# An attention layer with a hand-written step table: pv after the job in seven steps, a new job order, a max pass one step shorter ahead, and a prologue that fills rows from two DMA queues

## The chip, the cores and the metric

The kernel runs on one core of a Trainium2 chip. The metric is the time of one execution on the device in microseconds (us). Three runs of the kernel before gave 575.6 (median), 574.88 and 576.89.

## The reference

Eight batches of 512 tokens with 256 features, 16 heads of 16. Cut to what matters:

```python
xn = layer_norm(x, norm_w, norm_b)
q = (xn @ q_w + q_b).reshape(8, 512, 16, 16)
k = (xn @ k_w + k_b).reshape(8, 512, 16, 16)
att = einsum('bnhl,bmhl->bnmh', q, k)
att = att + (1.0 - mask.reshape(8, 1, 512, 1)) * -1000000.0
att = softmax(att, axis=2)
v = ((xn @ v_w + v_b) * mask[:, :, None]).reshape(8, 512, 16, 16)
y = einsum('bnmh,bmhl->bnhl', att, v).reshape(8, 512, 256)
e = silu(cond) @ emb_w + emb_b
scale, shift = split(e[:, None, :], 2, axis=2)
h = layer_norm(y, sb_norm_w, sb_norm_b) * (1.0 + scale) + shift
return x + silu(h) @ out_w + out_b
```

## The kernel before

A batch is 16 steps (`STEPS`): four groups of four heads, and for each group four chunks of 128 keys. The program runs ten bodies: body -1 is the prologue, body b computes the attention of batch b, body 8 is the tail. Each engine has its own instruction list, and semaphores tie them.

In a step TensorE does, in this order (`body`, L550): two score matmuls (`st_unit` 0 and 1, L442: the first pair), where it is due the turn of the maxima (`max_turn`, L434), the product of the exponentials of the step before with the values (`pv_step`, L459: "pv"; four heads side by side in four column strips of the array), four matmuls of the max pass (`max_quad`, L408: "maxima"; two at a time in two row strips), two further scores (the second pair), and one job (`job`, L499). The scores have two PSUM banks in turn, so a score waits until the exponential of the score two before it has been read (`exp_done`).

The softmax takes its row maxima from the max pass. It runs `MAX_LEAD` = 7 steps ahead of the scores with a cheaper product of split bf16 parts. VectorE reduces each pair of max banks (`max_pair`, L724). After four steps the sixteen columns of maxima of a group are turned by TensorE (`TURNS`: steps 1, 5, 9, 13), split into two bf16 parts (`split_max`, L759) and put by DMA into two rows of `q_rows` (`place_max`, L1140), so that the score matmul itself subtracts them.

`JOBS` names the sixteen jobs of a body as (kind, index, batch offset). Long jobs are the four projections of Q and K (`proj`), two value projections (`vproj`) and two output products (`outp`). Short ones are transposes: of the normed x (`xturn`), of y (`yturn`) and of the normed y (`hturn`). All use one bank, `job_ps`; a job waits until the last one has been read (`bank_freed`, L339).

ScalarE (L577) takes the four exponentials of a step and reads jobs: a projection twice, in full precision after the step's last exponential (`qk_full`) and rounded, as part 0, after the second exponential of the next step (`qk_parts`). It also copies `pv_ps` into `y_t` once in four steps. GpSimd subtracts part 0 (`take_rest`), VectorE rounds part 1 (`late_job`, whose places are in `LATE`), GpSimd makes part 2. SyncE issues all the DMAs (`spread`, L1101): it saves four copies of the parts to DRAM, fills three mask rows of each half, waits until the copies have landed and issues eight DMAs that fill the rows of K and Q for the group.

```python
JOBS = [
    ("yturn", 3, -1), ("xturn", 0, 1), ("xturn", 1, 1), ("proj", 0, 1),
    ("hturn", 0, -1), ("vproj", 0, 1), ("yturn", 0, 0), ("proj", 1, 1),
    ("hturn", 1, -1), ("vproj", 1, 1), ("yturn", 1, 0), ("proj", 2, 1),
    ("yturn", 2, 0), ("outp", 0, -1), ("outp", 1, -1), ("proj", 3, 1),
]
```

The prologue loads x and the weights, norms x, splits the mask into three bf16 parts on VectorE (`mask_rows`, L681), projects groups 0 to 3 of batch 0 and runs the max pass of its first seven steps. `keep_warm` issues matmuls on zeros in between.

Of the kernel before, what the change touches and what calls it, by code (L numbers as in the profile page):

```python
# [47 lines left out]
MAX_LEAD = 7  # L48
# [23 lines left out]
    ("yturn", 3, -1), ("xturn", 0, 1), ("xturn", 1, 1), ("proj", 0, 1),  # L72
    ("hturn", 0, -1), ("vproj", 0, 1), ("yturn", 0, 0), ("proj", 1, 1),
    ("hturn", 1, -1), ("vproj", 1, 1), ("yturn", 1, 0), ("proj", 2, 1),
    ("yturn", 2, 0), ("outp", 0, -1), ("outp", 1, -1), ("proj", 3, 1),
]

FIRST_JOBS = {1: 1, 2: 2, 3: 3, 5: 5, 6: 7, 7: 9, 8: 11, 15: 15}

TURNS = {1: 1, 5: 2, 9: 3, 13: 4}  # L80

LATE = {(2, 0): (15, -1), (5, 0): (3, 0), (7, 2): (4, 0), (9, 0): (7, 0), (10, 2): (8, 0), (13, 0): (11, 0)}
LATE_FIRST = {(5, 0): (3, 0), (8, 0): (7, 0), (12, 0): (11, 0)}
X_STAT = {(11, 0): (0,), (11, 2): (1,), (12, 2): (2,), (14, 2): (3,), (15, 2): (4,)}
Y_STAT = {(2, 1): (0,), (2, 2): (1,), (3, 0): (2, 3, 4)}
X_STAT_FIRST = 8


TURN_OF = {3: 1, 0: 5, 1: 9, 2: 13}
# [3 lines left out]
WARM_FIRST = {3: 4, 7: 6, 8: 2}  # L93
# [63 lines left out]
def attention_layer(nc, x, cond, mask, norm_w, norm_b, q_w, q_b, k_w, k_b, v_w, v_b,  # L157
                    emb_w, emb_b, sb_w, sb_b, out_w, out_b, out):
    with ExitStack() as ctx:
# [163 lines left out]
        def emptied(kind, i, batch):  # L323
            if kind == "proj":
                return part0_ready, NG * batch + i + 1
            if kind == "yturn":
# [6 lines left out]
                    ("proj", 2): st_ps[0][:, :], ("proj", 3): pv_ps[:, :]}  # L333
# [33 lines left out]

        block = ctx.enter_context(nc.Block())
# [3 lines left out]
        def _(pe):  # L372
# [14 lines left out]
            keep_warm(pv_ps, 7)  # L387
# [71 lines left out]
            def pv_step(b, t):  # L459
# [5 lines left out]
                if c == 0:  # L465

                    pe.wait_ge(v_ready, NG * b + g + 1)
                    wait(pe, yt_ready, NG * b + g)
                    if isinstance(b, int) and b == 0 and g == 0:

                        pe.wait_ge(part0_ready, NG)
# [27 lines left out]
            def job(t, b):  # L499
# [4 lines left out]
                if isinstance(b, int) and b == 0 and t == 1:  # L504

                    pe.wait_ge(setup_done, 1)
# [70 lines left out]
        def _(act):  # L577
# [15 lines left out]
            def read_job(b, t, half):  # L593
# [5 lines left out]
                if kind == "proj" and half == 1:  # L599
                    wait(act, copies_saved, 16 * COPIES * (NG * d + i))  # L600
# [31 lines left out]

            def yt_copy(b, t):
# [10 lines left out]
            def body(b):  # L644
                for t in range(STEPS):
# [7 lines left out]
                    read_job(b, t, 0)  # L653

# [21 lines left out]
        def _(dve):  # L676
            dve.memset(warm_in[:, :].bitcast(F32), 0.0).then_inc(warm_ready, 1)  # L677

            dve.memset(k_rows[0:HALF + P // 4, 0:NG // 2, :, :].bitcast(F32), TWO_ONES)

            def mask_rows():  # L681

                dve.wait_ge(mask_loaded, 16)
                dve.tensor_scalar(mask_bias[:, :], mask_in[:, :], -1.0, MASKED, ALU.add, ALU.mult).then_inc(setup_chain, 1)
                dve.wait_ge(setup_chain, 2)
                dve.tensor_copy(mask_parts[:, 0, :], mask_bias[:, :]).then_inc(setup_chain, 1)
                dve.wait_ge(setup_chain, 3)
                dve.tensor_tensor(mask_rest[:, 0, :], mask_bias[:, :], mask_parts[:, 0, :], ALU.subtract).then_inc(setup_chain, 1)
                dve.wait_ge(setup_chain, 4)
                dve.tensor_copy(mask_parts[:, 1, :], mask_rest[:, 0, :]).then_inc(setup_chain, 1)  # L690
                dve.wait_ge(setup_chain, 5)
                dve.tensor_tensor(mask_rest[:, 1, :], mask_rest[:, 0, :], mask_parts[:, 1, :], ALU.subtract).then_inc(setup_chain, 1)
                dve.wait_ge(setup_chain, 6)
                dve.tensor_copy(mask_parts[:, 2, :], mask_rest[:, 1, :]).then_inc(maskp_ready, 1)

                dve.memset(k_rows[0:HALF + P // 4, NG // 2:NG, :, :].bitcast(F32), TWO_ONES).then_inc(k_preset, 1)

            def silu_of_cond():
# [4 lines left out]
                dve.wait_ge(setup_chain, 1)  # L703
# [3 lines left out]
                                ).then_inc(mask_col_ready, 1)  # L707

# [189 lines left out]
            def body(b):  # L898
# [6 lines left out]
                for t in range(STEPS):  # L905
# [12 lines left out]
                    if t == 0 and isinstance(b, int) and b == 0:  # L918
                        embedding()
# [275 lines left out]
```

## Time and profile before

| | |
|---|---|
| median of three runs | 575.6 us |
| the profiled execution | 575.16 us |
| its span in the profile | 573.4 us |
| TensorE busy (PE) | 527.0 us, 92% |
| VectorE (DVE) | 414.9 us, 72% |
| ScalarE (ACT) | 366.3 us, 64% |
| GpSimd (POOL) | 197.2 us, 34% |
| granted TensorE clock, mean | 0.99 |

Busy times are sums over the span, and matmul ends are modelled, so a busy TensorE is not one at its peak. In the rows further down a line of a timeline gives start, length, engine, source line, operation, what is written and read, how many instructions were merged, and in brackets the idle time before them with what ended it.

### The profile page before, as it was taken

What the parts mean: (1) busy time and instruction counts of PE and PEld (TensorE: products, weight loads), DVE (VectorE), ACT (ScalarE), POOL (GpSimd) and SP (SyncE); (2) the same over time, 40 slices, a digit from 0 to 9 for tenths busy, and PEclk for the clock granted to TensorE, in tenths of its full rate; (3) what the DMA queues carried; (4) which work ended last, traced back from release to release, by engine and by line L of the source; (5) the groups of instructions that cost most, each with busy time, mean ns of one, the idle gap of its engine ahead of it and who ended that gap; (6) DMA issues with size and microseconds to landing.
All of it is one profiled execution on the core that took longest, in us unless ns stands there. A gap on an engine that the chain in (4) does not pass through costs nothing.

```text
span 573.4 us, 9986 instructions
## 1 busy us (share of the span) xinstructions
PE 527.0 (92%) x2841; PEld 194.4 (34%) x2845; DVE 414.9 (72%) x658; ACT 366.3 (64%) x674; POOL 197.2 (34%) x240
## 2 busy tenths in 40 slices
PE   7878999899999999999999999999999999988886
PEld 2433233223333233433333333433333333412243
DVE  7467767787687877887787877887777877787325
ACT  2302766677766877577766877577856877576851
POOL 9333203245322623255322623154322622132003
PEclk9979999999999999999999999999999999999999
DMA  5443243224424342424324342424424322421021
GB/s 144 164 131 92 82 134 95 86 83 123 120 75 149 90 123 86 127 78 128 111 76 148 93 124 80 130 76 128 120 65 147 95 91 76 152 59 49 1 74 37
DMA packets 55050, 57.95 MB, mean 101 GB/s; under 512 B 12376, under 2 KB 42200, under 8 KB 55024
## 3 DMA queue, kind: packets, MB, share of 16 engines
q1 hardware_dynamic: 55024, 57.64, 33.5%
q8 instruction: 12, 0.20, 0.1%
q14 instruction: 14, 0.11, 0.1%
HBM read 36.35 MB, written 21.00 MB: 100 GB/s over the span
## 4 chain that ended last, share of the span: by engine, by line
PE 65%; DVE 10%; ACT 8%; issue 8%; DMA 5%; SPq 3%; POOL 0%; ACTq 0%; DVEq 0%; POOLq 0%
PE pv_ps L475 19%; PE st_ps L456 14%; PE mx_ps L430 10%; PE job_ps L516 8%; ACT probs L591 7%; DVE negmax L735 7%; PE job_ps L523 4%; PE job_ps L546 4%; DMA qk_dram<-qk_parts 3%; SPq L1130 1%; PE pv_ps L377 1%; PE mx_ps L440 1%; SPq L1106 1%; DMA k_rows<-qk_dram 1%; ACT qk_parts L601 1%
## 5 line engine op out<-in xcount | busy, mean ns | idle before, releaser
L735 DVE TENSOR_REDUCE negmax<-mx_ps 128x2 f32<-128x1024 f32 x256 | 301.9, 1220 | 113.0 <-PE mx_ps L430 112.9
L591 ACT ACTIVATE probs<-st_ps 128x512 f32<-128x512 f32 x512 | 279.5, 604 | 111.3 <-PE st_ps L456 109.3
L456 PE MATMUL st_ps<-q_rows,k_rows 115*128 115x512 bf16 x512 | 166.7, 384 | 18.2 <-ACT probs L591 10.9
L475 PE MATMUL pv_ps<-probs,v_rows 128*32 128x512 f32 x1024 | 136.4, 605 | 1.0 <-ACT probs L591 1.0
L979 POOL TENSOR_TENSOR qk_rest<-qk_full,qk_parts 128x512 f32<-128x512 f32 x32 | 37.0, 1157 | 157.5 <-ACT qk_parts L601 157.5
L430 PE MATMUL mx_ps<-k_rows,q_rows 51*128 51x512 bf16 x512 | 80.3, 385 | 9.2 <-DMA k_rows<-qk_dram 6.6
L456 PEld LDWEIGHTS st_ps<-q_rows,k_rows 115*128 115x128 bf16 x512 | 39.5, 97 | 131.3 <-ACT probs L591 87.4
L988 POOL TENSOR_TENSOR qk_parts<-qk_rest,qk_parts 128x512 bf16<-128x512 f32 x32 | 37.0, 1157 | 66.4 <-DVE qk_parts L810 64.3
L430 PEld LDWEIGHTS mx_ps<-k_rows,q_rows 51*128 51x128 bf16 x512 | 16.4, 94 | 115.8 <-issue 68.9
L516 PE MATMUL job_ps<-x_norm_t,w_qk 128*128 128x512 f32 x112 | 52.7, 592 | 0.0
L612 ACT ACTIVATE qk_full<-job_ps,qkb_col 128x512 f32<-128x512 f32 x28 | 19.2, 687 | 23.8 <-PE job_ps L516 23.8
L475 PEld LDWEIGHTS pv_ps<-probs,v_rows 128*32 128x32 f32 x1024 | 20.2, 107 | 38.2 <-issue 33.2
L998 POOL TENSOR_TENSOR v_biased<-v_plain,vb_row 128x256 f32<-128x256 f32 x32 | 23.2, 726 | 23.8 <-ACT v_plain L623 12.7
L523 PE MATMUL job_ps<-w_v,x_norm_t 128*128 128x256 f32 x120 | 28.4, 379 | 0.0
L954 POOL TENSOR_TENSOR x_rstd<-x_vareps,exponent 128x4 f32<-128x4 f32 x8 | 8.2, 1022 | 56.5 <-DVE x_vareps L750 56.4
L516 PEld LDWEIGHTS job_ps<-x_norm_t,w_qk 128*128 128x128 f32 x112 | 21.2, 189 | 17.5 <-issue 13.5
L546 PE MATMUL job_ps<-w_o,h_t 128*128 128x256 f32 x112 | 26.5, 379 | 0.0
L534 PE MATMUL job_ps<-ident,y_t 128*128 128x128 f32 x128 | 19.8, 277 | 6.1 <-ACT y_t L642 6.1
L523 PEld LDWEIGHTS job_ps<-w_v,x_norm_t 128*128 128x128 f32 x120 | 22.8, 190 | 4.9 <-issue 0.5
L546 PEld LDWEIGHTS job_ps<-w_o,h_t 128*128 128x128 f32 x112 | 21.2, 190 | 4.2
L1003 POOL TENSOR_TENSOR v_rows<-v_biased,mask_now 128x256 f32<-128x256 f32 x32 | 19.6, 612 | 3.9 <-POOL v_biased L998 2.0
L377 PE MATMUL pv_ps<-warm_in 128*128 128x512 bf16 x59 | 19.2, 469 | 1.6 <-DVE warm_in L677 1.3
(113 smaller groups left out, 405.0 us busy)
## 6 DMA issues: line engine op xcount, KB each, us to landing
qk_dram<-qk_parts SPq DMA_DIRECT2D x128, 128.0 KB
q_rows<-qk_dram SPq DMA_DIRECT2D x128, 96.0 KB
k_rows<-qk_dram SPq DMA_DIRECT2D x128, 96.0 KB
x_in<-in_x SPq DMA_DIRECT2D x16, 256.0 KB, 2.9
x_res<-in_x SPq DMA_DIRECT2D x8, 512.0 KB, 4.0
out<-out_sb SPq DMA_DIRECT2D x16, 256.0 KB, 2.7
w_e<-in_L_cond_emb_w SPq DMA_DIRECT2D x1, 1024.0 KB, 5.8
k_rows<-mask_dram SPq DMA_DIRECT2D x64, 6.0 KB
```

The source lines that it names most:

```text
L377: pe.matmul(ps[:, :], warm_in[:, 0:P], warm_in[:, :], start=True, stop=True)
L430: pe.matmul(mx_ps[j][:, half, :], q_rows[base:base + ROWS_MX, g, h, c * P:(c + 1) * P], k_rows[base:base + ROWS_MX, g, h, :], start=True, ...
L456: pe.matmul(st_ps[u % ST_BANKS][:, :], k_rows[0:ROWS_ALL, g, h, c * P:(c + 1) * P], q_rows[0:ROWS_ALL, g, h, :], start=True, stop=True).th ...
L475: mm = pe.matmul(pv_ps[VW * h:VW * (h + 1), :], v_rows[:, c, g * GH + h, :], probs[:, t % P_SLOTS, h, :], start=(c == 0), stop=(c == CH - ...
L516: mm = pe.matmul(ps, w_qk[:, k, i, :], x_norm_t[:, k, :], start=(k == 0), stop=(k == KD - 1))
L523: mm = pe.matmul(ps[:, c * D:(c + 1) * D], x_norm_t[:, k, tok:tok + P], w_v[:, k, :], start=(k == 0), stop=(k == KD - 1))
L546: mm = pe.matmul(ps[:, c * D:(c + 1) * D], h_t[:, k, tok:tok + P], w_o[:, k, :], start=(k == 0), stop=(k == KD - 1))
L591: act.activation(probs[:, t % P_SLOTS, h, :], st_ps[u % ST_BANKS][:, :], ACT.Exp).then_inc(exp_done, 1)
L735: dve.tensor_reduce(by_pair[:, :, j, c], mx_ps[j][:, :, :], AXIS_X, ALU.max, negate=True).then_inc(max_done, 1)
L979: pool.tensor_tensor(qk_rest[:, :], qk_full[:, :], qk_parts[:, 0, :], ALU.subtract).then_inc(rest_ready, 1)
L988: pool.tensor_tensor(qk_parts[:, 2, :], qk_rest[:, :], qk_parts[:, 1, :], ALU.subtract).then_inc(part2_ready, 1)
L998: pool.tensor_tensor(v_biased[:, :, :], v_plain[:, :, g * GC:(g + 1) * GC], vb_row[:, g * GC:(g + 1) * GC].unsqueeze(1).broadcast_to((P, C ...
```

## The change

Five things are changed at once.

- In the steps of the new set `APART` (1, 3, 5, 7, 9, 11, 15) TensorE does first pair, maxima, second pair, job, pv. The other steps keep the old order.
- The jobs are in another order. Projection 3 of a batch moves from step 15 of the body before to step 0 of its own; the other jobs come one step later, and transpose of y group 2 comes last. `LATE`, `X_STAT`, `Y_STAT` and `TURNS` follow.
- The max pass runs six steps ahead instead of seven.
- SyncE's list: the two mask DMAs come after all four saves, and so, where the turn comes last, ahead of the max rows.
- Prologue: the first save no longer waits for presets; VectorE alone makes the parts of the first projection; the rows of groups 0 and 1 are filled half by SyncE's queue and half by ScalarE's; so is the first pair of max rows; the mask's parts come ahead of the condition's silu; projection 3 of batch 0 leaves the prologue; other counts of warming matmuls. The embedding's VectorE work moves to the start of step 0.

```diff
-MAX_LEAD = 7
+MAX_LEAD = 6
 JOBS = [
-    ("yturn", 3, -1), ("xturn", 0, 1), ("xturn", 1, 1), ("proj", 0, 1),
...
+    ("proj", 3, 0), ("yturn", 3, -1), ("xturn", 0, 1), ("xturn", 1, 1),
+    ("proj", 0, 1), ("hturn", 0, -1), ("vproj", 0, 1), ("yturn", 0, 0),
+    ("proj", 1, 1), ("hturn", 1, -1), ("vproj", 1, 1), ("yturn", 1, 0),
+    ("proj", 2, 1), ("outp", 0, -1), ("outp", 1, -1), ("yturn", 2, 0),
 ]
+APART = (1, 3, 5, 7, 9, 11, 15)
-TURNS = {1: 1, 5: 2, 9: 3, 13: 4}
+TURNS = {2: 1, 6: 2, 10: 3, 14: 4}
...
+        def fill_rows(engine, i, half):
+            at = HALF * half + PARTS
+            for own in range(2):
+                heads = slice(PAIRS * own, PAIRS * (own + 1))
+                for side, rows in enumerate((q_rows, k_rows)):
+                    engine.dma_start(rows[at:at + ROWS_PROD, i, heads, :].rearrange("p h t -> p (h t)"),
+                                     copies(i, side, own, half != own)).then_inc(rows_filled[i], 16)
...
                     st_unit(b, t, 0)
                     st_unit(b, t, 1)
-                    max_turn(b, t)
-                    pv_step(b, t)
+                    if t not in APART:
+                        max_turn(b, t)
+                        pv_step(b, t)
                     max_quad(b, t)
...
                     st_unit(b, t, 2)
                     st_unit(b, t, 3)
                     job(t, b)
+                    if t in APART:
+                        pv_step(b, t)
...
                 if kind == "proj" and half == 1:
+                    if isinstance(d, int) and d == 0 and 0 < i < 3:
+                        fill_half(i - 1)
...
+            def fill_half(i):
+                if i == 0:
+                    act.wait_ge(q_preset, 3)
+                    act.wait_ge(k_preset, 1)
+                act.wait_ge(copies_saved, 16 * COPIES * (i + 1))
+                fill_rows(act, i, 1)
+
+            def place_first_max():
+                act.wait_ge(max_split, 1)
+                act.dma_start(max_row(0, 1), max_parts[:, 0, 1:2, :]).then_inc(max_filled[0], 16)
...
+            def first_parts():
+                dve.wait_ge(part0_ready, 1)
+                dve.tensor_tensor(qk_rest[:, :], qk_full[:, :], qk_parts[:, 0, :], ALU.subtract).then_inc(rest_ready, 1)
+                dve.wait_ge(rest_ready, 1)
+                dve.tensor_copy(qk_parts[:, 1, :], qk_rest[:, :]).then_inc(part1_ready, 1)
+                dve.wait_ge(part1_ready, 1)
+                dve.tensor_tensor(qk_parts[:, 2, :], qk_rest[:, :], qk_parts[:, 1, :], ALU.subtract).then_inc(part2_ready, 1)
...
-            sp.wait_ge(mask_saved, 16)
-            sp.wait_ge(q_preset, 3)
-            sp.wait_ge(k_preset, 1)
...
                 if exists(d):
+                    save(2, 1, part1_ready)
+                    save(3, 2, part2_ready)
+                    if first and i == 0:
+                        sp.wait_ge(mask_saved, 16)
+                        sp.wait_ge(q_preset, 3)
+                        sp.wait_ge(k_preset, 1)
+                    if first and i == 2:
+                        sp.wait_ge(k_preset, 2)
                     for half in range(2):
                         sp.dma_start(k_rows[HALF * half:HALF * half + PARTS, i, PAIRS * half:PAIRS * (half + 1), :],
...
-                    save(2, 1, part1_ready)
...
-                    save(3, 2, part2_ready)
```

How it moves the instructions of TensorE: first the old list, from a value projection (L523) over the next step with the transpose of y (L534) to the step of a projection (L516). L456 are scores, L475 pv, L430 maxima.

```order
L523 MATMUL job_ps<-w_v,x_norm_t 128x256 x4
L456 MATMUL st_ps<-q_rows,k_rows 128x512 x2
L475 MATMUL pv_ps<-probs,v_rows 32x512 x4
L430 MATMUL mx_ps<-k_rows,q_rows 128x512 x4
L456 MATMUL st_ps<-q_rows,k_rows 128x512 x2
L534 MATMUL job_ps<-ident,y_t 128x128 x4
L456 MATMUL st_ps<-q_rows,k_rows 128x512 x2
L475 MATMUL pv_ps<-probs,v_rows 32x512 x4
L430 MATMUL mx_ps<-k_rows,q_rows 128x512 x4
L456 MATMUL st_ps<-q_rows,k_rows 128x512 x2
L516 MATMUL job_ps<-x_norm_t,w_qk 128x512 x2
```

The same piece of the new list (L542 value projection, L478 scores, L452 maxima, L553 transpose of y, L494 pv, L535 projection):

```order
L542 MATMUL job_ps<-w_v,x_norm_t 128x256 x4
L478 MATMUL st_ps<-q_rows,k_rows 128x512 x2
L452 MATMUL mx_ps<-k_rows,q_rows 128x512 x4
L478 MATMUL st_ps<-q_rows,k_rows 128x512 x2
L553 MATMUL job_ps<-ident,y_t 128x128 x4
L494 MATMUL pv_ps<-probs,v_rows 32x512 x4
L478 MATMUL st_ps<-q_rows,k_rows 128x512 x2
L494 MATMUL pv_ps<-probs,v_rows 32x512 x4
L452 MATMUL mx_ps<-k_rows,q_rows 128x512 x4
L478 MATMUL st_ps<-q_rows,k_rows 128x512 x2
L535 MATMUL job_ps<-x_norm_t,w_qk 128x512 x2
```

Only the maxima now stand between the two pairs of the step with the short job, and pv has gone behind that job.

On SyncE, the first group of the prologue before:

```order
L1096 DMA mask_dram<-mask_parts 8x1536 [waits maskp_ready]
L1106 DMA qk_dram<-qk_parts 8x16x512 [waits k_preset,part0_ready,q_preset,mask_saved]
L1106 DMA qk_dram<-qk_parts 8x16x512 [waits part0_ready]
L1113 DMA k_rows<-mask_dram 3x2x512 x2
L1106 DMA qk_dram<-qk_parts 8x16x512 [waits part1_ready]
L1106 DMA qk_dram<-qk_parts 8x16x512 [waits part2_ready]
L1130 DMA q_rows<-qk_dram 48x1x1024 [waits copies_saved]
```

and now:

```order
L1147 DMA mask_dram<-mask_parts 8x1536 [waits maskp_ready]
L1154 DMA qk_dram<-qk_parts 8x16x512 [waits part0_ready] x2
L1154 DMA qk_dram<-qk_parts 8x16x512 [waits part1_ready]
L1154 DMA qk_dram<-qk_parts 8x16x512 [waits part2_ready]
L1173 DMA k_rows<-mask_dram 3x2x512 [waits k_preset,q_preset,mask_saved]
L1173 DMA k_rows<-mask_dram 3x2x512
L383 DMA q_rows<-qk_dram 48x1x1024 [waits copies_saved]
```

The waits for the presets have moved from the first save to the mask rows; the row at the end stands for eight DMAs before, for four now, with the other four on ScalarE.

## Rows read from the trace of the kernel before

**Rows 1.** The page, part 4: shares of the chain that ended last.

```profile
PE 65%; DVE 10%; ACT 8%; issue 8%; DMA 5%; SPq 3%; POOL 0%; ACTq 0%; DVEq 0%; POOLq 0%
```

**Rows 2.** Timeline of TensorE, a step with a short and one with a long job.

```profile
247.94 0.28 PE L440 MATMUL mx_ps<-ident,negmax 128*16 128x128 f32 x1
248.15 1.07 PE L475 MATMUL pv_ps<-probs,v_rows 128*32 128x512 f32 x8
249.15 0.60 PE L430 MATMUL mx_ps<-k_rows,q_rows 51*128 51x512 bf16 x4
249.68 0.60 PE L456 MATMUL st_ps<-q_rows,k_rows 115*128 115x512 bf16 x2
250.12 0.60 PE L529 MATMUL job_ps<-ident,x_norm 128*128 128x128 f32 x4
250.76 0.88 PE L456 MATMUL st_ps<-q_rows,k_rows 115*128 115x512 bf16 x2
251.57 1.06 PE L475 MATMUL pv_ps<-probs,v_rows 128*32 128x512 f32 x8
...
256.97 1.88 PE L516 MATMUL job_ps<-x_norm_t,w_qk 128*128 128x512 f32 x4
258.69 0.60 PE L456 MATMUL st_ps<-q_rows,k_rows 115*128 115x512 bf16 x2
259.21 1.06 PE L475 MATMUL pv_ps<-probs,v_rows 128*32 128x512 f32 x8
```

**Rows 3.** Timeline of ScalarE, the same steps and one after a value projection.

```profile
250.11 1.08 ACT L591 ACTIVATE probs<-st_ps 128x512 f32<-128x512 f32 x2 [1.59 <-PE st_ps L456]
...
258.89 0.69 ACT L612 ACTIVATE qk_full<-job_ps,qkb_col 128x512 f32<-128x512 f32 x1 [0.85 <-PE job_ps L516]
259.47 1.07 ACT L591 ACTIVATE probs<-st_ps 128x512 f32<-128x512 f32 x2
260.43 0.70 ACT L601 ACTIVATE qk_parts<-job_ps,qkb_col 128x512 bf16<-128x512 f32 x1
...
267.20 0.59 ACT L623 COPY v_plain<-job_ps 128x512 f32<-128x512 f32 x1 [0.86 <-PE job_ps L523]
```

**Rows 4.** VectorE's timeline; waits, in us in total, times, longest.

```profile
249.60 2.36 DVE L735 TENSOR_REDUCE negmax<-mx_ps 128x2 f32<-128x1024 f32 x2 [0.60 <-PE mx_ps L430]
...
PEld mx_ps L440 <- DVE negmax L735: 11.4, 31, 0.7
```

**Rows 5.** TensorE's timeline: the first scores of batch 1 and of batch 7.

```profile
114.88 0.60 PE L456 MATMUL st_ps<-q_rows,k_rows 115*128 115x512 bf16 x2
...
500.41 0.60 PE L456 MATMUL st_ps<-q_rows,k_rows 115*128 115x512 bf16 x2
```

**Rows 6.** TensorE's timeline: first and seventh maxima of the prologue, first scores.

```profile
31.81 1.04 PE L430 MATMUL mx_ps<-k_rows,q_rows 51*128 51x512 bf16 x4 [5.90 <-DMA k_rows<-qk_dram]
...
49.16 0.75 PE L430 MATMUL mx_ps<-k_rows,q_rows 51*128 51x512 bf16 x4
...
52.64 0.60 PE L456 MATMUL st_ps<-q_rows,k_rows 115*128 115x512 bf16 x2
```

**Rows 7.** Prologue: timelines of VectorE, ScalarE, SyncE's queue; DMA issues (us to landing last).

```profile
15.36 0.68 DVE L692 TENSOR_TENSOR mask_rest<-mask_rest,mask_parts 8x512 f32<-8x512 f32 x1
16.07 0.41 DVE L694 CAST mask_parts<-mask_rest 8x512 bf16<-8x512 f32 x1
...
16.40 0.68 ACT L601 ACTIVATE qk_parts<-mx_ps,qkb_col 128x512 bf16<-128x512 f32 x1
...
18.89 1.34 SPq L1106 DMA_DIRECT2D qk_dram<-qk_parts  x2
21.10 1.20 SPq L1106 DMA_DIRECT2D qk_dram<-qk_parts  x2
24.62 0.63 SPq L1130 DMA_DIRECT2D q_rows<-qk_dram  x1
...
q_rows<-max_parts SPq DMA_DIRECT2D x64, 4.0 KB, 2.2
```

More of the change, by code:

```diff
@@ L366, in last_body, with copies, max_row @@
             return isinstance(b, int) and b == B
+        def copies(i, side, own, rest):
+            heads = slice(side * GH + PAIRS * own, side * GH + PAIRS * (own + 1))
+            of = qk_dram[i, rest:rest + PARTS, :, heads, :].rearrange("s l h t -> l s (h t)")
+            return of if side == 0 else of[:, ::-1]
+        def fill_rows(engine, i, half):
[5 more added lines that the diff above has]
+                                     copies(i, side, own, half != own)).then_inc(rows_filled[i], 16)
+        def max_row(g, part):
+            return q_rows[ROW_MAX + part:ROW_MAX + part + 1, g, :, :].rearrange("p h (c t) -> p (h c) t", t=P)
         block = ctx.enter_context(nc.Block())
@@ L653, in body @@
                     read_job(b, t, 0)
+                if isinstance(b, int) and b == -1:
+                    place_first_max()
                 if last_body(b):
@@ L902, in body @@
                     half_norm(x_in, x_norm, x_negmean, x_rstd, x_rstd_ready, x_norm_ready, 0)
+                    mask_rows()
                     silu_of_cond()
-                    mask_rows()
+                    first_parts()
+                    dve.memset(k_rows[0:HALF + P // 4, NG // 2:NG, :, :].bitcast(F32), TWO_ONES).then_inc(k_preset, 1)
                 for t in range(STEPS):
                     read_job(b, t - 1)
+                    if t == 0 and isinstance(b, int) and b == 0:
+                        embedding()
                     late_job(b, t, 0)
@@ L909, in body @@
                     split_max(b, t)
+                    late_job(b, t, 1)
                     max_pair(b, t, 0)
@@ L917, in body @@
                         dve.tensor_copy(cond_t[:, :, :], st_ps[1][:, 0:KE * B].rearrange("p (k b) -> p k b", b=B)).then_inc(cond_ready, 1)
[L918 to L921 removed]
+                    if last_body(b) and 0 < t < 3:
+                        last_stats(t - 1)
                 if last_body(b):
@@ L1039, in body @@
                                      ).then_inc(mod_ready, 1)
-                take_rest(b, 0, 1)
-                take_part2(b, 0, 1)
+                if not (isinstance(b, int) and b == -1):
+                    take_rest(b, 0, 1)
+                    take_part2(b, 0, 1)
                 if exists(b - 1):
@@ L1107, in save @@
                                  ).then_inc(copies_saved, 16)
+                first = isinstance(d, int) and d == 0
                 if exists(d):
@@ L1124, in spread @@
                     sp.wait_ge(copies_saved, 16 * COPIES * (n + 1))
-                    for half in range(2):
-                        at = HALF * half + PARTS
-                        for own in range(2):
-                            heads = slice(PAIRS * own, PAIRS * (own + 1))
-                            for side, rows in enumerate((q_rows, k_rows)):
-                                sp.dma_start(rows[at:at + ROWS_PROD, i, heads, :].rearrange("p h t -> p (h t)"),
-                                             copies(i, side, own, half != own)).then_inc(rows_filled[i], 16)
-            def copies(i, side, own, rest):
-                heads = slice(side * GH + PAIRS * own, side * GH + PAIRS * (own + 1))
-                of = qk_dram[i, rest:rest + PARTS, :, heads, :].rearrange("s l h t -> l s (h t)")
-                return of if side == 0 else of[:, ::-1]
+                    for half in range(1 if first and i < 2 else 2):
+                        fill_rows(sp, i, half)
             def place_max(b, i):
@@ L1145, in place_max @@
                 sp.wait_ge(max_split, NG * d + g + 1)
-                for part in range(2):
-                    sp.dma_start(q_rows[ROW_MAX + part:ROW_MAX + part + 1, g, :, :].rearrange("p h (c t) -> p (h c) t", t=P),
-                                 max_parts[:, g % 2, part:part + 1, :]).then_inc(max_filled[g], 16)
+                for part in range(1 if isinstance(d, int) and d == 0 and g == 0 else 2):
+                    sp.dma_start(max_row(g, part), max_parts[:, g % 2, part:part + 1, :]).then_inc(max_filled[g], 16)
             def body(b):
@@ L1161, in body @@
                 spread(b, 1, 1, False)
-                spread(b, 2, 1, False)
+                spread(b, 2, 1, isinstance(b, int) and b == -1)
                 for i in range(2):
```

58 lines of the change are left out of this document (26 added, 32 removed).

## The prediction

> **What bounds the kernel now.** I read the page's chain first: TensorE holds most of the path that ends last [rows 1], so I went to its timeline in the middle of the run. Three numbers of it carry everything below. A step with a long job (projection or output product, 1.72 us from its start to the next score pair) has no gap: first pair 0.53, pv 1.00, maxima 0.54, second pair 0.44, job 1.72, together 4.23 us. A step with a short job (four transposes) takes 3.42 us from pv to pv, 248.15 to 251.57 [rows 2], and there TensorE waits: the next first pair starts 0.64 after the short job, though the job, with the same 0.60 in its row as a pair, needs some 0.46, and holds its second score back again. The reason is ScalarE: an exponential starts 0.43 after its score matmul, and the score that reuses the bank starts 0.65 after that exponential [rows 2, 3]. Two scores thus can't follow two others in under 1.08 us. The third thing is a wait on VectorE: a pair of maxima takes it 2.36 us from 0.45 after the first maxima matmul, and the turn of the maxima in the step after a short job waits for it [rows 2, 4].
>
> Eight long and eight short steps a batch should give 8 x 4.23 + 8 x 3.42 + 4 turns x 0.21 = 62.0 us. Measured between the first scores of batch 1 and batch 7 is (500.41 - 114.88) / 6 = 64.26 [rows 5]; the 2.2 above it I lay to the short steps after a projection, where ScalarE has two copies of the job to make [rows 3] and the turn that follows waits for VectorE [rows 4].
>
> **The steady batch.** I write an apart step (maxima between the pairs, pv after the job) with the measured distances, p = 0 at its first pair.
> - After a projection, ScalarE first copies the job: its first exponential starts 0.78 after the pair (258.69 to 259.47), the second 0.48 later, then comes the second copy at 1.74, done at 2.43 [rows 2, 3]. Scores three and four start at 1.43 and 1.91. The short job shares the job's bank, so it waits for that second copy: 2.49. Then pv at 3.04 (0.46 of job and 0.09 as from pair to pv) and the next pair at 4.04. Three such steps (1, 5, 9): 12.12.
> - After a value projection the copy is 0.1 shorter [rows 3] and there is no second one: scores at 1.33 and 1.81, job 2.04, pv 2.59, next pair 3.59. Two (7, 11): 7.18.
> - After an output product ScalarE has nothing to copy: 1.08, 1.56, job 1.79, end 3.34 (step 15).
> - Step 3 follows a short step, so its own first pair is stretched and the copy of the turned x comes before its exponentials: 3.87. Step 2, in the old form with a turn: 3.36.
> - Eight long steps 33.84, and the turns of steps 6, 10 and 14 now stand openly, 3 x 0.21 = 0.63.
>
> Sum 64.4 by batch, against 64.26: **no gain**. What goes: the waits of turns on VectorE and the two copies of ScalarE in one step. What comes: the exponentials that are late because a long job was just copied now hold the second pair, where earlier pv and maxima (1.54) lay between. Only 0.54 of maxima lies there now. Over six batches +0.5 us. The prices with no row are the distance from pv to a score (I take the 1.00 of pv to maxima; it lies between the pure 0.85 of four passes of 0.21, half the 0.44 of a pair, and 1.15) and from a pair to maxima (0.53 as to pv; 0.44 to 0.60). Both ends, for 49 apart steps in seven bodies: -11 to +11 us, but the ends need both errors in one direction; half of that is likely.
>
> Here a rule speaks against the change. From pair to pv is 0.53, from pair to a full-array job 0.44 [rows 2], so a change of array form costs 0.09. An apart step has four such changes where the old one had three. The Trainium skill (TensorEngine Tiling (Array Packing), Key Properties) says that changing the tiling mode drains the engine. By that rule the fourth change costs 49 x 0.09 = 4.4 us more than a count that ignores it; my distances hold it already, and two of the four lie inside the wait on exponentials.
>
> **The max pass six ahead.** It leaves one step less between turn and scores. For the group whose turn is in step 14 I count from the turn: VectorE reads the output product and copies part 1 (done +0.75), GpSimd's part 2 till +2.05, SP saves it (0.65), issues the two mask rows (0.75, now ahead of the maxima's), then the two max rows, the second at +4.1; it lands 2.2 later [rows 7], at +6.3. The scores that wait for it stand at 4.44 - 0.53 + 3.34 = +7.25. Slack 0.95 us; at the three other groups 2.4. Cost nothing. The rows of K and Q keep some 19 us from part 0 to their first maxima, for the 14.7 that the prologue shows (17.1 to 31.81).
>
> **Prologue.** The first maxima matmul waits for the rows of group 0 until 31.81 [rows 6]. Before it: part 0 ready at 17.1, SP held until 18.89 for presets, the last copies issued by 22.30, the wait to 24.62 for them to land, eight issues of 0.63 each on SP to 29.7, and 2.1 more [rows 6, 7]. Now nothing holds the first save; VectorE, not GpSimd, makes parts 1 and 2 (0.68 + 0.41 + 0.68 by the operations of equal width [rows 7]) after the mask's chain, which ended at 16.5, and three small operations of the condition (an estimate of 1.4 from the 0.41 to 0.68 of these rows): part 2 at 16.5 + 1.4 + 1.8 = 19.7 at worst, 18.2 if the mask chain gains the time it starts sooner; I take 19.0. Save till 19.7, landed 22.0, four issues on each queue till 24.5, landed 26.6, with 0.4 for eight transfers side by side: **27.0**, 4.8 us sooner (bounds 2.5 and 6). ScalarE's queue is now blocked through its four issues, and the copy of projection 1 behind them comes at 24.4 instead of 24.63, so nothing is late.
> Then the old program had seven sets of maxima (31.81 to 49.16 for six distances, 2.9 each) and projection 3, scores at 52.64 [rows 6]. Now five distances: 27.0 + 14.5 = 41.5, plus the old 3.48 less the projection's 1.72, plus 0.4 for a copy of part 1 that now lies between the sets: scores at **43.7**, 8.9 sooner.
>
> **Batch 0.** Projection 3 returns in its step 0, after the embedding's operations on VectorE: 4.4 us. Steps without a job: apart 3.23 (1, 5, 9), 13 to 15 3.15, 4.1 and 3.4. With the others as above: 4.4 + 9.69 + 3.36 + 3.87 + 12.69 + 8.88 + 7.18 + 10.65 = 60.7, against 114.88 - 52.64 = 62.24 [rows 5, 6]: 1.5 sooner. **Batch 7** has one projection more and one step of maxima more, and gains about that in its seven steps without job, where an apart step lets pv run inside the score's wait: nothing, give or take 1.5.
>
> **Sum.** -8.9 - 1.5 + 0.5 = -9.9. The profiled execution took 575.16 (span 573.4), so 565.2; the median of the runs, 575.6, lies 0.4 above it, so 565 to 566. I say **565**.
>
> **Rivals.**
> 1. The apart steps gain (0.20). For it: the maxima and two changes of form lie where TensorE waits anyway, and pv after the job gives ScalarE time to read it. Against it: a copied job moves the first exponential from 0.43 to 0.78 [rows 3]. If each is 0.17 better than I count (the 3.42 of the old form in place of 3.59), 49 x 0.17 = 8.3: 557.
> 2. The apart steps lose (0.12): scores after pv start 0.15 later than 1.00, each change of form in the open. 49 x 0.15 = 7.4: 572.5. The skill's rule on draining above is this one's reason.
> 3. The prologue's rows come no sooner (0.10): both queues feed the same transfers, or VectorE reaches part 2 late behind the mask. First maxima at 31: 569.
> 4. Slower than before (0.05): the max rows land late and the first scores of every group wait, with everything behind them on TensorE. Decided by the landing time: at 2.2 nothing, from 3.1 the group of step 14, from 4.6 all four. At 5 us: 1.85 + 3 x 0.4 = 3 us a batch, 7 x 3 = 21: 586. Against it: nothing but larger transfers takes so long here.
> The forecast itself (560 to 570) has 0.53.
>
> **Numbers.** What a measurement can tell from no change is about 0.3%, 573.9 to 577.3. Faster 0.90: forecast, rivals 1 and 3, and most of 2. Same 0.04 and slower 0.06: rivals 2 and 3 together, and 4. Range 555 to 573: rival 1 and the greater part of 2 are in.
>
> **What would show it.** First maxima matmul near 27, first score near 43.7, first score of batch 1 near 104.4; score to score between batches 1 and 7 64.4 each. In an apart step after a projection the pair distance 4.04, after a value projection 3.59, with the second pair waiting on exponentials; the turn no longer waiting on VectorE. A steady batch under 63.5 or over 65.5 makes the account of apart steps wrong; any wait of scores on max rows makes the lead's wrong.

## The result, and the profile after

The changed kernel takes **566.97 us** (median of four runs, 565.78 to 569.3) against 575.49 for the kernel before beside it: ratio 0.9854, 95% interval 0.9815 to 0.9893, so some 8.5 us faster. The ratios leave out three slow executions of about 660 us at a mean clock of 0.75, one of a variant below and two of the kernel before beside the second group of variants. The forecast was 565 in a range of 555 to 573. The profiled execution is the longest of the four (569.3, span 567.6 at a mean granted clock of 0.991; the others have spans of 564.1 to 566.1), and why it is longer is part of what follows.

The page of the kernel after, part 4, answers [rows 1]:

```profile
PE 70%; ACT 14%; DVE 7%; issue 6%; POOL 1%; ACTq 1%; DMA 1%; POOLq 0%; SPq 0%; DVEq 0%
```

DMA and SyncE's queue have nearly left the chain (8% before, 1% now, and 1% for ScalarE's queue). The chain of the kernel before in order of time, as the profile draws it, shows where the 29 us of DMA in it lay: 11 in the prologue, 5 in the last batch, and in each of the batches 0 to 5 a piece of 2.0 like this one, the landing of a saved part:

```profile
102.43 2.03 DMA qk_dram<-qk_parts
```

No such piece is left in the chain of the kernel after. So the prologue is a part of what left the chain, and not all of it. ScalarE has come up from 8% to 14%, and the page of waits, each with its total, its count and its longest, says where:

```profile
PE st_ps L478 <- ACT probs L613: 14.6, 46, 0.7
PE st_ps L415 <- DVE cond_silu L741: 2.9, 1, 2.9
PE job_ps L558 <- ACT qk_parts L625: 2.2, 12, 0.2
PE job_ps L553 <- ACT qk_parts L625: 1.7, 7, 0.3
```

The first of these waits in the kernel before, and then the wait of the turn of the maxima in the kernel after:

```profile
PE st_ps L456 <- ACT probs L591: 10.9, 25, 0.8
PEld mx_ps L462 <- DVE negmax L781: 0.9, 2, 0.7
```

Scores waited for exponentials 25 times and now wait 46 times. The weight load of the turn waited 31 times for VectorE [rows 4] and now waits twice.

TensorE's timeline of the kernel after (start, duration, engine, line, operation; in brackets the idle time before it and its releaser): first maxima and first scores of the prologue, first scores of batches 1 and 7. These answer [rows 5, 6].

```profile
28.81 0.61 PE L452 MATMUL mx_ps<-k_rows,q_rows 51*128 51x512 bf16 x4
...
44.35 0.60 PE L478 MATMUL st_ps<-q_rows,k_rows 115*128 115x512 bf16 x2
...
105.31 0.61 PE L478 MATMUL st_ps<-q_rows,k_rows 115*128 115x512 bf16 x2
...
492.96 0.61 PE L478 MATMUL st_ps<-q_rows,k_rows 115*128 115x512 bf16 x2
```

A steady batch takes (492.96 - 105.31) / 6 = 64.61, batch 0 takes 60.96. A step after a projection and the one behind it, in the same timeline; they answer [rows 2]:

```profile
109.54 0.60 PE L478 MATMUL st_ps<-q_rows,k_rows 115*128 115x512 bf16 x2
110.07 0.60 PE L452 MATMUL mx_ps<-k_rows,q_rows 51*128 51x512 bf16 x4
110.97 0.88 PE L478 MATMUL st_ps<-q_rows,k_rows 115*128 115x512 bf16 x2 [0.30 <-ACT probs L613]
112.04 0.66 PE L553 MATMUL job_ps<-ident,y_t 128*128 128x128 f32 x4 [0.19 <-ACT qk_parts L625]
112.62 1.06 PE L494 MATMUL pv_ps<-probs,v_rows 128*32 128x512 f32 x8
113.62 0.61 PE L478 MATMUL st_ps<-q_rows,k_rows 115*128 115x512 bf16 x2
114.07 0.27 PE L462 MATMUL mx_ps<-ident,negmax 128*16 128x128 f32 x1
114.27 1.06 PE L494 MATMUL pv_ps<-probs,v_rows 128*32 128x512 f32 x8
...
116.25 0.60 PE L548 MATMUL job_ps<-ident,x_norm 128*128 128x128 f32 x4
116.89 0.88 PE L478 MATMUL st_ps<-q_rows,k_rows 115*128 115x512 bf16 x2
```

The reader should see four things. The second pair waits for an exponential, since only 0.54 us of maxima lie before it. The short job waits for ScalarE's second copy of the projection. From pair to pair the step takes 4.08, forecast 4.04. And the turn at 114.07 stands without a wait, 0.45 after the pair. These are the steps of batch 1; in batches 2 to 6 step 1 takes 4.23, not 4.08, because its two waits on ScalarE are longer (0.38 and 0.26).

The prologue holds what the forecast did not look for. TensorE's and the queues' timeline of the kernel after:

```profile
16.36 0.59 PE L415 MATMUL st_ps<-ident,cond_silu 8*128 8x8 f32 x4 [2.92 <-DVE cond_silu L741]
...
16.88 3.78 PE L542 MATMUL mx_ps<-w_v,x_norm_t 128*128 128x256 f32 x8
...
20.45 2.83 PE L535 MATMUL mx_ps<-x_norm_t,w_qk 128*128 128x512 f32 x4
...
21.45 0.63 SPq L383 DMA_DIRECT2D q_rows<-qk_dram  x1
...
23.12 1.89 PE L542 MATMUL job_ps<-w_v,x_norm_t 128*128 128x256 f32 x8
...
23.32 0.69 ACT L636 ACTIVATE qk_full<-mx_ps,qkb_col 128x512 f32<-128x512 f32 x1 [2.03 <-PE mx_ps L535]
...
23.40 0.64 ACTq L383 DMA_DIRECT2D q_rows<-qk_dram  x1
```

After the wait of 2.92 us for the condition, eight matmuls of the value projection take 3.78, twice the 1.89 of the same eight at 23.12: the granted clock is 0.50 from 15.6 to 22.3, the lower of the two levels, and 1.00 behind it. Projection 1 ends late, ScalarE's copy of it with it, and the row transfers that ScalarE issues behind that copy start at 23.40, 1.95 after SyncE's.

Where all the time of each profiled execution lies (first scores of batch 1 and 7 as above; "from batch 7" is what follows the first scores of batch 7). The last column has the times in us of those executions of each kernel, profiled or not, whose mean granted clock was 1.0, so that the clock plays no part in them:

| kernel | first maxima | first scores | first scores of batch 1 | a batch, mean of six | from batch 7 | span | times at mean clock 1.0 |
|---|---|---|---|---|---|---|---|
| before | 31.81 | 52.64 | 114.88 | 64.26 | 73.0 | 573.4 | none |
| after | 28.81 | 44.35 | 105.31 | 64.61 | 74.6 | 567.6 | 565.78, 566.12 |
| late condition | 27.91 | 43.44 | 104.40 | 64.61 | 73.0 | 565.1 | six, 566.15 to 567.5 |
| one queue | 29.26 | 44.79 | 105.88 | 64.61 | 73.0 | 566.6 | 568.3 |
| no apart step | 27.76 | 43.29 | 105.77 | 63.79 | 74.0 | 562.5 | 563.54 |
| apart 1, 5, 9 | 26.85 | 42.38 | 103.93 | 64.13 | 73.7 | 562.4 | 563.32, 563.38, 564.11 |
| lead 7, no apart | 27.84 | 45.78 | 107.71 | 62.65 | 73.7 | 557.3 | 556.52 |
| lead 7, apart 3, 7, 11, 15 | 27.26 | 49.82 | 110.20 | 62.92 | 73.9 | 561.6 | 559.67, 560.01, 560.23 |
| lead 7, late condition | 27.14 | 45.09 | 107.26 | 62.83 | 73.7 | 558.0 | 558.11, 559.5, 559.71 |

In the kernel after, 1.5 of the last stretch is the lower clock again (granted clock 0.50 from 513.9 to 517.2, eight pv matmuls in 1.94 instead of 1.06 at 514.49).

### The profile page after: what moved, and what is told of

The parts are those of the page before. It is cut to its first block, busy times and chain, and to the rows that moved or that the text cites. A ratio compares the mean times of both kernels' runs of the same rounds, so it can differ in the third digit from the quotient of the medians.

```text
span 567.6 us, 10004 instructions
## 1 busy us (share of the span) xinstructions
PE 526.0 (93%) x2845; PEld 195.1 (34%) x2848; DVE 419.8 (74%) x661; ACT 372.2 (66%) x674; POOL 194.3 (34%) x237
## 4 chain that ended last, share of the span: by engine, by line
PE 70%; ACT 14%; DVE 7%; issue 6%; POOL 1%; ACTq 1%; DMA 1%; POOLq 0%; SPq 0%; DVEq 0%
PE pv_ps L494 22%; PE st_ps L478 15%; ACT probs L613 10%; PE job_ps L535 9%; PE mx_ps L452 7%; PE job_ps L542 5%; PE job_ps L565 4%; DVE negmax L781 4%; PE job_ps L553 3%; ACT qk_parts L625 2%; PE job_ps L558 2%; PE pv_ps L399 1%; PE mx_ps L542 1%; PE mx_ps L462 1%; PE job_ps L548 1%
## 5 line engine op out<-in xcount | busy, mean ns | idle before, releaser
L478 PE MATMUL st_ps<-q_rows,k_rows 115*128 115x512 bf16 x512 | 166.5, 385 | 21.4 <-ACT probs L613 14.6
L494 PE MATMUL pv_ps<-probs,v_rows 128*32 128x512 f32 x1024 | 137.0, 608 | 0.0
L478 PEld LDWEIGHTS st_ps<-q_rows,k_rows 115*128 115x128 bf16 x512 | 39.5, 97 | 169.2 <-ACT probs L613 119.7
L452 PE MATMUL mx_ps<-k_rows,q_rows 51*128 51x512 bf16 x512 | 81.2, 382 | 3.3 <-DVE negmax L781 1.4
L535 PE MATMUL job_ps<-x_norm_t,w_qk 128*128 128x512 f32 x116 | 54.7, 593 | 0.6 <-DVE mod_half L768 0.6
L452 PEld LDWEIGHTS mx_ps<-k_rows,q_rows 51*128 51x128 bf16 x512 | 16.7, 94 | 87.9 <-issue 62.9
L494 PEld LDWEIGHTS pv_ps<-probs,v_rows 128*32 128x32 f32 x1024 | 20.3, 108 | 37.5 <-issue 32.2
L535 PEld LDWEIGHTS job_ps<-x_norm_t,w_qk 128*128 128x128 f32 x116 | 21.9, 189 | 19.1 <-issue 14.0
L542 PE MATMUL job_ps<-w_v,x_norm_t 128*128 128x256 f32 x120 | 28.4, 379 | 0.0
L542 PEld LDWEIGHTS job_ps<-w_v,x_norm_t 128*128 128x128 f32 x120 | 22.8, 190 | 4.9 <-issue 0.5
L679 ACT COPY y_t<-pv_ps 128x512 f32<-128x512 f32 x32 | 18.8, 586 | 7.0 <-PE pv_ps L494 6.0
L856 DVE CAST qk_parts<-qk_rest 128x512 bf16<-128x512 f32 x31 | 13.1, 423 | 12.2 <-POOL qk_rest L1029 12.2
L553 PE MATMUL job_ps<-ident,y_t 128*128 128x128 f32 x128 | 19.7, 275 | 2.5 <-ACT qk_parts L625 1.7
```

The lines of the kernel that those rows point to most:

```text
L452: pe.matmul(mx_ps[j][:, half, :], q_rows[base:base + ROWS_MX, g, h, c * P:(c + 1) * P], k_rows[base:base + ROWS_MX, g, h, :], start=True, ...
L478: pe.matmul(st_ps[u % ST_BANKS][:, :], k_rows[0:ROWS_ALL, g, h, c * P:(c + 1) * P], q_rows[0:ROWS_ALL, g, h, :], start=True, stop=True).th ...
L494: mm = pe.matmul(pv_ps[VW * h:VW * (h + 1), :], v_rows[:, c, g * GH + h, :], probs[:, t % P_SLOTS, h, :], start=(c == 0), stop=(c == CH - ...
L535: mm = pe.matmul(ps, w_qk[:, k, i, :], x_norm_t[:, k, :], start=(k == 0), stop=(k == KD - 1))
L542: mm = pe.matmul(ps[:, c * D:(c + 1) * D], x_norm_t[:, k, tok:tok + P], w_v[:, k, :], start=(k == 0), stop=(k == KD - 1))
L553: mm = pe.transpose(ps[:, c * P:(c + 1) * P], y_t[:, c * P:(c + 1) * P], ident[:, :])
```

## The experiments

The medians of the kernel before differ a little from one chip to the next (575.49, 576.32, 577.38), so kernels of different groups are compared by their ratios. The first group is the four kernels with a median of 576.32 beside them (no apart step, apart steps in the old order, apart steps after projections, seven steps ahead); the other four have 577.38. The changed kernel itself was not run again in either.

**The change without its apart steps.**

```diff
-APART = (1, 3, 5, 7, 9, 11, 15)
+APART = ()
```

> The changed kernel with an empty set of apart steps: every step keeps first pair, turn, pv, maxima, second pair, job. Theory A (the apart form costs, because the exponentials come late behind the copy of a long job, and only 0.54 us of maxima lies in front of the second pair): steps 3, 7, 11 and 15 fall back from 3.88, 3.58, 3.58 and 3.37 to 3.42, the pairs of steps 1+2, 5+6 and 9+10 stay within 0.2; a steady batch 63.8 instead of 64.6, the whole some 5 us faster than the changed kernel: 561 to 562 us. Theory B (the apart form gains by running maxima inside the wait on exponentials, and the steady batch is long for another reason): 570 us or more.

Measured: 564.2 us, ratio 0.9785 (0.9752 to 0.9818), against 0.9854 (0.9815 to 0.9893) with them: the intervals just touch, so the steps have to carry the reading. A steady batch takes 63.79, as theory A had it, 0.82 shorter than with the apart steps. The total of 561 to 562 was missed by 2, because batch 0 is 1.5 longer and the last stretch 0.9 longer (against the two variants that kept their clock there, 73.0). In batch 0 the steps 1, 5 and 9 carry no job, ScalarE has nothing to copy, and each of them with its successor is 0.7 shorter in the apart form; in the steady batch the form loses. The steps 7, 11 and 15 did not fall back to 3.42 but to 3.14 or 3.23; the long step behind each grew from 4.23 to 4.50 instead, its first pair held longer. Step and successor together change by 0.2 in steps 3, 7 and 11, and by 0.1 the other way in step 15. The price of the old form behind a projection is a wait of the turn, in TensorE's timeline of this kernel:

```profile
110.19 0.60 PE L478 MATMUL st_ps<-q_rows,k_rows 115*128 115x512 bf16 x2
...
112.69 0.65 PE L553 MATMUL job_ps<-ident,y_t 128*128 128x128 f32 x4
113.33 0.88 PE L478 MATMUL st_ps<-q_rows,k_rows 115*128 115x512 bf16 x2
114.58 0.28 PE L462 MATMUL mx_ps<-ident,negmax 128*16 128x128 f32 x1 [0.38 <-DVE negmax L781]
114.79 1.07 PE L494 MATMUL pv_ps<-probs,v_rows 128*32 128x512 f32 x8
...
117.53 0.88 PE L478 MATMUL st_ps<-q_rows,k_rows 115*128 115x512 bf16 x2
```

and its row of waits:

```profile
PE mx_ps L462 <- DVE negmax L781: 9.4, 25, 0.4
```

The step after the projection takes 3.14 and the next one, with the turn, 4.20: 7.34 together. With the apart form it is 109.54 to 116.89 above, 7.35. So in batch 1 what the apart form loses in step 1 it gets back in step 2. In batches 2 to 6, where step 1 takes 4.23, the two take 7.49 and lose 0.15.

**Three apart steps in the old order of jobs.** Here pv and maxima are parted in the kernel before, in three of its short steps without a turn: one behind another short step, two behind a value projection.

```diff
+APART = (2, 6, 10)
...
-                    max_turn(b, t)
-                    pv_step(b, t)
+                    if t not in APART:
+                        max_turn(b, t)
+                        pv_step(b, t)
...
+                    if t in APART:
+                        pv_step(b, t)
```

> The kernel before with the apart form in steps 2, 6 and 10 alone, old job order, old lead, old prologue. Theory A: step 2 (behind a short step) +0.45, steps 6 and 10 (behind a value projection) +0.17 each, +0.8 us a batch, over seven bodies +5.5: 581 us. Theory B: no slower than before, 570 to 575.

Measured: 581.63 us, ratio 1.007 (1.0044 to 1.0096), slower than the kernel before. A steady batch takes (505.20 - 116.66) / 6 = 64.76, 0.50 more, 0.17 for each apart step, where theory A had 0.8. Step 2 cost not 0.45 but 0.20 with its successor, since the long step behind it became shorter (4.23 for 4.50). The total hit the 581 of theory A by luck: at the same mean clock of 0.988 the executions are 579.19 to 580.58 against 575.4 to 576.67 for the kernel before, some 4 us; the median is 5.3 higher because more executions here had a clock below that. The form by itself costs time where it takes no wait away.

**Apart steps only after projections.**

```diff
-APART = (1, 3, 5, 7, 9, 11, 15)
+APART = (1, 5, 9)
```

> The changed kernel with the apart form only in the steps after a projection (1, 5, 9). Theory A: these three are near neutral, since a wait of the turn on VectorE goes and one of the job on the second copy stays: within 1.5 us of the kernel with no apart steps, 561 to 563. Theory B: between that kernel and the changed one, nearer the changed one.

Measured: 564.03 us, ratio 0.9781 (0.9747 to 0.9815), the same as with none, as theory A said; the 561 to 563 it gave is missed by 1. A steady batch is 64.13: 0.34 over the kernel with none, 0.11 for each of the three steps, and the other four cost 64.61 - 64.13 = 0.48, 0.12 each. So the steps after a projection and the others cost about the same. The profiled executions are level because here the first scores come 0.9 sooner and batch 0 is 0.9 shorter (61.55). In this execution the prologue came at the full clock, and the first maxima stand where the forecast had them:

```profile
21.50 0.64 ACTq L383 DMA_DIRECT2D q_rows<-qk_dram  x1
...
26.85 0.61 PE L452 MATMUL mx_ps<-k_rows,q_rows 51*128 51x512 bf16 x4 [0.85 <-DMA k_rows<-qk_dram]
...
103.93 0.60 PE L478 MATMUL st_ps<-q_rows,k_rows 115*128 115x512 bf16 x2 [1.30 <-DMA q_rows<-max_parts]
```

The last row is the first scores of batch 1: they waited 1.30 for the rows of maxima, where the forecast had slack.

**Seven steps ahead again, no apart step, new jobs and new prologue.**

```diff
-MAX_LEAD = 6
+MAX_LEAD = 7
-APART = (1, 3, 5, 7, 9, 11, 15)
+APART = ()
-TURNS = {2: 1, 6: 2, 10: 3, 14: 4}
+TURNS = {1: 1, 5: 2, 9: 3, 13: 4}
-TURN_OF = {3: 2, 0: 6, 1: 10, 2: 14}
+TURN_OF = {3: 1, 0: 5, 1: 9, 2: 13}
```

> As the first (no apart steps), and the max pass seven steps ahead again, its turns one step sooner (1, 5, 9, 13). If the shorter lead is worth one set of maxima in the prologue and nothing in the steady batch, this is 2.0 to 3.5 us slower than the first, and the steady batch is the same within 0.1. If the shorter lead costs waits later (max rows late, turns in the open), it is less than 2 us slower or even faster.

Measured: **559.38 us**, ratio 0.9689 (0.9651 to 0.9727), the fastest of all and faster than the change by 1.7%, with intervals that do not touch. TensorE's timeline of it:

```profile
111.94 0.60 PE L478 MATMUL st_ps<-q_rows,k_rows 115*128 115x512 bf16 x2
112.38 0.27 PE L462 MATMUL mx_ps<-ident,negmax 128*16 128x128 f32 x1
112.58 1.06 PE L494 MATMUL pv_ps<-probs,v_rows 128*32 128x512 f32 x8
...
115.38 0.88 PE L478 MATMUL st_ps<-q_rows,k_rows 115*128 115x512 bf16 x2
...
118.80 0.88 PE L478 MATMUL st_ps<-q_rows,k_rows 115*128 115x512 bf16 x2
```

The turn stands right behind the first pair after a long job, when VectorE is done. Two steps take 3.44 and 3.42, 6.86 where six ahead takes 7.34 or 7.35. This is the best of the four places: steps 9 and 10 gain 0.4, the turn in step 13 takes 0.4 out of step 14, and steps 5 and 6 gain nothing. Its rows of waits, to be held against those of the kernel without apart steps:

```profile
PE st_ps L478 <- ACT probs L613: 6.3, 12, 0.8
...
PE mx_ps L452 <- DMA k_rows<-qk_dram: 3.0, 6, 0.8
PE mx_ps L462 <- DVE negmax L781: 1.5, 3, 0.9
```

The 9.4 us on VectorE are 1.5. A new wait has come: 3.0 us on rows of K, which the max pass now wants one step sooner. Half of it lies in batch 0; batches 2 and 3 have most of the rest, and the first scores of batch 3 wait 0.72 for rows of maxima. Those two batches take 63.5 and 63.0, the others 62.1 to 62.5. So dropping one step of lead costs 63.79 - 62.65 = 1.14 a batch on average, and it saves 43.29 against 45.78, 2.5, once. Between batches without such a wait (63.84 and 62.4) it is 1.4.

**The same with four apart steps**, in short steps without a turn: `APART = (3, 7, 11, 15)` in the kernel just described.

> The kernel with lead seven and no apart steps, with the apart form in steps 3, 7, 11 and 15 (with turns in 1, 5, 9 and 13 no other short steps are free). If the apart form costs by late exponentials whatever the lead: +0.46, +0.16, +0.16 and about -0.05, so 0.7 to 0.8 us a batch over 62.35, and some 5 us slower than without: 564. If its cost came from the shorter lead: within 1 us of 559.4.

Measured: 561.02 us, ratio 0.9717 (0.9685 to 0.9748). A steady batch is 62.92, 0.27 more, 0.07 for each apart step; the sign is as before, the size about half, and the totals forecast by either theory (564, or within 1 of 559.4) were both missed. The interval overlaps that of the kernel without apart steps. At a mean clock of 1.0 the times are 559.67 to 560.23 against 556.52, and 558.11 to 559.71 for the last kernel below, which was run beside this one. The profiled execution ran part of its prologue at the lower clock (maxima of 1.04 at 42.02 and 46.74), so its first scores aren't compared.

**Later condition work in the prologue of the change.** The transposes of the condition stand behind the value projections, and more warm matmuls follow.

```diff
-TURN_STEP = 4
+TURN_STEP = 7
-WARM_FIRST = {2: 5, 8: 10}
+WARM_FIRST = {2: 5, 8: 26}
```

> The changed kernel with the transposes of the condition moved behind the second value projection (step 7 of the prologue in place of 4), and 26 warming matmuls in place of 10 after projection 2. Theory P (TensorE's idle time of 2 to 3 us before those transposes lets the clock fall, and the slow value projection and projection 1 hold ScalarE's copy, behind which its half of the row DMAs stands): TensorE has no gap of over 1 us between the first projection and the first maxima, ScalarE issues its rows at 21.5 as SyncE does, first maxima at 26.0 to 27.0 in every execution, the whole 1 to 2.5 us faster than the changed kernel: 564.5 to 566, with a smaller spread. Rival: the first maxima follow the landing of SyncE's own rows and stay near 28.8; no change.

Measured: 567.11 us, ratio 0.9825 (0.9795 to 0.9854). TensorE doesn't wait in front of the value projection and the matmuls keep the higher clock; all six executions have a mean clock of 1.0, where the change had 1.0 in two of four:

```profile
13.63 1.89 PE L542 MATMUL mx_ps<-w_v,x_norm_t 128*128 128x256 f32 x8
...
27.91 0.60 PE L452 MATMUL mx_ps<-k_rows,q_rows 51*128 51x512 bf16 x4 [1.08 <-DMA k_rows<-qk_dram]
```

The first maxima come 0.9 before those of the profiled execution of the change, but behind the 26.85 of an execution at the full clock. The transfers set the time here: the second issue took 1.25 on ScalarE's queue and 1.33 on SyncE's, where the execution above has 0.79 and 0.60. Why they took longer is not shown. The forecast of 564.5 to 566 is missed and the ratio lies inside the interval of the change. The lower clock in the prologue is gone, but the kernel isn't measurably faster: at a mean clock of 1.0 the change itself took 565.78 and 566.12.

**All eight row transfers on SyncE's queue again.**

```diff
-                        fill_half(i - 1)
+                        pass
...
-                    for half in range(1 if first and i < 2 else 2):
+                    for half in range(2):
```

> The changed kernel with all eight row DMAs of groups 0 and 1 on SyncE's queue again. By the issue time of 0.63 us each, the last goes out at 26.5 instead of 24 (or of 26.2 where ScalarE's half was late): first maxima at 28.8 to 29.2, so 0 to 2 us slower than the changed kernel: 567 to 569. Rival (eight transfers at once only share the same engines): no difference, and first maxima equally soon.

Measured: 568.13 us, ratio 0.9849 (0.9818 to 0.9881); the first maxima at full clock:

```profile
29.26 0.61 PE L452 MATMUL mx_ps<-k_rows,q_rows 51*128 51x512 bf16 x4 [3.13 <-DMA k_rows<-qk_dram]
```

29.26 against 26.85 for two queues, also at full clock. Of these 2.4 us, 0.5 is that SyncE's first row transfer went out later here (21.91 against 21.42). From that issue to the first maxima it is 7.35 with one queue, 5.4 to 5.5 in three executions where ScalarE reached its transfers in time, 6.5 in the one with the long issues, and 7.36 in the profiled one of the change. So the second queue is worth 1.9 us at best, for four issues of 0.6 fewer in a row, and nothing when ScalarE is 1.95 late. In the time of the kernel it doesn't stand clear of the change (0.9849 and 0.9854). The other half of the gain of the prologue (31.81 to 29.26) comes without it.

**The fastest version with the later condition work**: both edits together.

> Lead seven, no apart steps, and the prologue of the first kernel of this set. If both gains are independent: 559.4 less 1 to 2.5, 557 to 558.5 us. If the first scores are held by something else with lead seven (rows of group 2, needed one step sooner): 559 or more.

Measured: 559.61 us, ratio 0.971 (0.9668 to 0.9753). No difference from the kernel with lead seven alone can be told. Its span is the longer by 0.7, with first scores 0.7 sooner and batches 0.2 longer on average (one took 64.1).

## Why the prediction was right, and where it was not

- **Prologue.** Forecast first maxima at 27.0 and first scores at 43.7; 26.85 and 42.38 in the execution that kept its clock, 28.81 and 44.35 in the profiled one of the change. The rows were costed well [rows 6, 7]. The stretch between the two was not: 16.7 forecast, 15.5 measured. Two of the six distances behind the 2.9 ran partly at the lower clock (maxima of 1.04 at 31.81 [rows 6] and at 35.02), and the last maxima stand 1.63 before the scores, not 2.16. That 43.7 lies so near the 44.35 of the profiled execution is luck: first maxima 1.8 later, the stretch 1.2 shorter. Missing was that the condition's transposes now find TensorE idle: the old prologue put warm matmuls there, the new one does not, and when the clock falls there, projection 1 ends late and ScalarE's half of the transfers with it. The forecast said that nothing on ScalarE is late; it did not count that ScalarE's copy of projection 1 stands ahead of its issues.
- **Batch 0.** Forecast 60.7, measured 60.96, with step 0 at 4.63 for 4.4.
- **The steady batch.** Forecast 64.4, measured 64.61. By its steps, pair to pair: 4.08 after a projection (4.04), 3.58 after a value projection (3.59), 3.88 in step 3 (3.87), 3.27 in step 2 (3.36), 3.37 in step 15 (3.34), and 4.36 in steps 6 and 10, the turn 0.13 instead of 0.21. Step 14 took 4.66 for 4.44. That is batch 1; in batches 2 to 6 the errors are three of one size, 4.23 for 4.04 in step 1, 4.40 for 4.23 in step 13 and 4.61 for 4.44 in step 14. The distance that no row had, pv to scores, is 1.00 (112.62 to 113.62), as taken.
- **The rule on draining.** A fourth change of form would cost 0.09, it was said, and no more. Pair to maxima is 0.53, job to pv 0.54 to 0.58, pv to scores 1.00, as to maxima. The Trainium skill (TensorEngine Tiling (Array Packing), Key Properties) says that changing the mode drains the array; this trace agrees with no more than those 0.09, and the second rival, which wanted 0.15 more for each step, did not come.
- **Batch 7.** Forecast nothing; 73.0 before, and 73.0 in the two variants of the change with the same steps at full clock (late condition, one queue).
- **The sum.** Forecast -9.9. In the profiled execution -5.8: -8.3 first scores, -1.3 batch 0, +2.1 steady, +1.6 at the end, where the clock fell. By the medians -8.5.
- **Wrong: "Cost nothing" for the max pass six ahead.** I looked only at the max rows. There it held in the change, with nothing to spare: once, at the first scores of batch 1, the weight load waited 0.8 for them while TensorE lost nothing, and in the variant with steps 1, 5 and 9 the scores themselves waited 1.30 there. A wait of scores on max rows was the forecast's own sign against this part. But one step less moves the turn from behind a long job to behind a short one. It costs 1.14 a batch by the pair of kernels without apart steps, 5.2 of span in all, ratio 0.9785 against 0.9689. It didn't show in my sum because I had summed the new batch step by step and had laid the apart form's part and the lead's part together. That total came out by the steps, not by luck; the cause given for it did not.
- **Incomplete: what the 2.2 us above 62.0 in the batch before are.** I gave them to the short steps after a projection and to the turn. By the steps of batch 3 these make some 1.0: the two steps with both copies take 3.47 where a short step behind a long one takes 3.14 without a wait, and three of the turns cost 0.12 or 0.13 beyond their 0.21. Two rows that I didn't use hold most of the rest. The first is from the page of waits, the second from TensorE's timeline of the kernel before:

```profile
PE job_ps L534 <- ACT y_t L642: 6.1, 16, 0.8
...
105.55 0.39 PE L430 MATMUL mx_ps<-k_rows,q_rows 51*128 51x512 bf16 x2 [0.28 <-DVE max_parts L772]
```

  The transpose of y waited for ScalarE's copy of it 16 times, 0.7 in a steady batch, and the maxima of step 13 waited 0.28 for VectorE's second part of the maxima. In the new order of jobs one wait of 0.8 is left of the first kind, and one of 0.5, in the prologue, of the second.

So a change that was forecast as "no gain in the steady batch" is three in one, which nearly cancel. From the kernel before to the one with seven steps ahead and no apart step, a batch falls from 64.26 to 62.65 (-1.6, six times -9.7, the new order of jobs with what follows it on VectorE and SyncE; the new prologue gives another 6.9 to the first scores, 52.64 to 45.78). Six steps ahead gives back 1.14 a batch, and 0.8 in batch 0 and at the end, and takes 2.5 off the prologue: +5.2. Seven apart steps give back 0.82 a batch and save 1.5 in batch 0 and 0.9 at the end: +2.6, from 562.5 to the 565.1 of the variant with late condition work, which has the steps of the change and kept its clock. What stays open: whether the row wait of 3.0 us in the fastest kernel can be taken away too; that wasn't tried. Nor was the old order run with the new prologue, and SyncE's new list was never undone alone, so the share of the order is worked out from the steady batches and isn't shown by a run.

## What to carry to other kernels

When a change bundles several edits and its steady state comes out level, undo each alone: here the level sum hid a gain of 1.6 us a batch and two losses of 1.1 and 0.8. When a stage is moved by one step in a hand-made order, ask what now stands directly ahead of each of its instructions, as well as whether its data are there in time: the row of the turn's wait on VectorE [rows 4] already named the price. And where TensorE waits in a prologue, look at what hangs on the matmuls behind the wait: here transfers of another engine did. A filler kept the clock up in all six executions, but it made the kernel no faster than the change's own executions at full clock, so its gain is an even time and not a shorter one.

## What the runs showed of the hardware

The granted clock in the prologue fell in some executions and stayed in others, with the same code. After idle times of 2.92, 3.05 and 3.09 us before the condition's transposes the value projection's eight matmuls took 3.78, 2.84 and 2.72; after 1.40, 1.95 and 2.70 they took 1.99. The idle time itself varied because the projection before it started between 11.44 and 13.13, in four executions when the load of a bias had landed, in the other two behind ScalarE's copy of the turned x. Six executions don't tell what decides; the kernel without the idle time kept 1.89. Executions of the change spread over 565.78 to 569.3, those of the later condition work over 566.15 to 567.5.
